# Two edits to a two-layer attention and expert network: expert inputs by a list of tokens per slot, and the turning of the near-bias table beside the first maxima

## The chip, the cores and the metric

The program runs on one core of a Trainium2 chip. Its time is the device time of one execution in microseconds (us); the time of the kernel before is 2062.14 us, the median of three runs (2062.14, 2062.99, 2052.34). The engines are TensorE (PE in the rows, PEld for its weight loads), VectorE (DVE), ScalarE (ACT), GpSimd (POOL) and SyncE (SP, which here issues DMAs); each runs its own stream of instructions in order, and they meet through semaphores.

## The reference

A network of two layers on x of shape (4, 1024, 128), 4096 tokens of 128 numbers. Layer 0 is a state-space scan and a dense mixture of 16 experts. Layer 1 is an attention with a relative-position bias and a second sublayer that holds a causal attention and a routed mixture of 16 experts. Cut to what the change touches:

```
# layer 1, attention: 16 heads of 8 numbers, bias by bucketed distance key - query
att = einsum('bhqd,bhkd->bhqk', q, k) / sqrt(8) + compute_bias(rel_emb, t, t)
o   = softmax(att) @ v;  out = o.reshape(b, t, 128) @ Wo.T

# layer 1, second sublayer, after its causal attention: T = 4096, E = 16, C = 2*ceil(T/E) = 512
hidden = resid + (ctx @ o_w + o_b)
xt     = layer_norm(hidden, ln2_w, ln2_b).reshape(T, 128)
logits = xt @ router_w;  probs = softmax(logits)
top1   = argmax(probs);  top2 = argmax(logits without top1)
loc1   = cumsum(m1) - 1; loc2 = cumsum(m2) - 1 + m1.sum()     # m1, m2: one-hot of top1, top2
m1, m2 = m1 * (loc1 < C), m2 * (loc2 < C)                     # over 512 a choice is dropped
xin    = einsum('tec,td->ecd', dispatch, xt)                  # (16, 512, 128): slots of the experts
h      = gelu(xin @ fc1_w + fc1_b)                            # 128 -> 512
eout   = (h @ fc2_w + fc2_b) * 0.8                            # 512 -> 128
moe    = einsum('tec,ecd->td', combine, eout)                 # g1*slot of top1 + g2*slot of top2
return hidden + moe                                           # then x + gate * this
```

## The kernel before

**The order of the program.** Modulate; scan; first mixture (from about 120 to 460 us); modulate; the biased attention, whose names begin with `ba_`; modulate; the causal attention, whose names begin with `ca_`; routing; the second mixture. Most stages are a Block: every engine has its own list in it, and the next Block begins for all of them together. `projection` has no Block of its own: it returns five functions (one per engine) that `attend` calls at the head of its own Block (`first.tensor(pe)` and so on).

**The biased attention.** `projection` runs over 8 chunks of 512 tokens. For each, TensorE computes q and k (L734) and v (L739) into PSUM, VectorE and ScalarE split q and k into three bfloat16 parts, and SyncE stores these in DRAM (`qk_parts`) and loads them back in another layout (`qop`, `kop`, loads at L833). The kernel applies the position bias as a factor on the exponentials: near the diagonal it comes from the table `rb_near` (128 rows by 16 heads by 384), and elsewhere it is constant. The table is built with its rows in reverse. `projection` turns it in 12 pieces of 512 columns: TensorE multiplies a piece by a flipped identity (L747) into PSUM bank 6 or 7, VectorE copies it back over itself (L810, semaphore `near_kept`), one or two pieces per chunk. At the end of the projection TensorE and GpSimd wait until all 12 are back.

`attend` first finds each row's maximum, then the scores. A "turn" of the maxima is one head group of one block of queries: two matmuls of 512 columns (L1149), a maximum by VectorE over both (L1234). 24 turns (`BEFORE_FIRST`) are put ahead of the first scores (L1175); after that a planner written in Python (`plan`) mixes the rest with the scores, the exponentials by ScalarE (L1267), GpSimd's product with `rb_near` (L1313) and the value matmuls (L1194). The maxima use banks 0 to 3, the scores 4 to 6, the values 7. The causal attention runs the same two functions, without table and turns.

**Routing (`route`, one Block).** VectorE makes layer-norm statistics; VectorE and ScalarE write the normalised rows `xt` (plain, without ln2's weight); TensorE turns them and multiplies by the router; VectorE finds the two choices, counts places with TensorE's help, and forms for each choice a row number `row` between 0 and 8191 (expert times 512 plus place), or a number above for a dropped one. The first choice's numbers are cast at L1705 into `cs_to` (semaphore `to_ready`), then the second's. ScalarE copies `xt` for the second choice (L1626); GpSimd writes a token's own result row into the 129th column of both copies (L1632). Then `send_copies` (L1725): GpSimd scatters 32 tiles of 128 rows for each choice, 64 indirect DMAs, into `expert_rows_in`, which has 129 columns and was zeroed in the first mixture. While it sends, VectorE makes the weights `g`, multiplies `hidden` by the gate and adds it to x (L1717, eight operations).

**Second mixture (`experts`, a Block of its own).** SyncE waits for all 64 sends and then loads the 512 rows of one expert after another, two in flight. TensorE turns the rows (L1830), multiplies up (L1839: 4 x (128x512)) and down (L1848: 16 pairs of 128x128); ScalarE applies gelu; VectorE takes the row numbers out of the 129th column and applies ln2 behind the turn, adds the second bias into `ex_eo` (L1918). In TensorE's order expert e+1's turn stands ahead of expert e's up, and expert e's down behind expert e+1's up. GpSimd gives each expert's 512 results back with four indirect scatters into `expert_rows_out` (L1769). Weights of an expert are 256 KB twice, loaded by SyncE two experts ahead. Behind the last give SyncE reads both results of each token back, ScalarE, VectorE and GpSimd weigh and add them, and SyncE stores the output.

Of the kernel before, what the change touches and what calls it, by code (L numbers as in the profile page):

```python
# [13 lines left out]
F32 = mybir.dt.float32  # L14
BF16 = mybir.dt.bfloat16
I32 = mybir.dt.int32
# [4 lines left out]
P = 128  # L21
# [20 lines left out]
CAP = 2 * (TOK // E)  # L42
KEEP = 1.0 - 0.2
# [339 lines left out]
def first_mixture(nc, k, m, by_distance):  # L383
# [8 lines left out]
    with ExitStack() as c:  # L392
# [39 lines left out]
        with nc.Block() as block:  # L432
            @block.sync
            def _(sp):
# [4 lines left out]
                sp.dma_start(k.rows_in[0:E * CAP, 0:D].rearrange("(p a) d -> p a d", p=P),  # L439
                             zero[:, 0:D].unsqueeze(1).broadcast_to([P, E * CAP // P, D])).then_inc(cleared, 16)  # L440
                sp.dma_start(k.rows_in[0:E * CAP, D:D + 1].bitcast(I32).rearrange("(p a) b -> p (a b)", p=P), m["unused_rows"],
                             allow_slow_non_contiguous=True).then_inc(cleared, 16)

# [7 lines left out]
                sp.wait_ge(cleared, (3 + 2) * 16)  # L451
# [224 lines left out]
def projection(nc, k, a):  # L676
# [10 lines left out]
    FLIPS = H * NEAR // CH  # L687
# [12 lines left out]
    def flips(i):  # L700

        return range(i * FLIPS // NCH, (i + 1) * FLIPS // NCH)

# [3 lines left out]
    if not a.causal:  # L707
        flipped, near_kept = nc.alloc_semaphore("rb_flipped"), nc.alloc_semaphore("rb_near_kept")
        near = a.near[:].rearrange("p h q -> p (h q)")

# [15 lines left out]
    def tensor(pe):  # L726
        pe.wait_ge(halved, 2)
        for i in range(NCH):
# [13 lines left out]
            if not a.causal:  # L742
# [10 lines left out]
        if not a.causal:  # L753
            pe.wait_ge(near_kept, FLIPS)

# [18 lines left out]
    def gpsimd(pool):  # L774
# [10 lines left out]
        if not a.causal:  # L785
            pool.wait_ge(near_kept, FLIPS)

    def vector(dve):
# [5 lines left out]
        for i in range(NCH):  # L794
# [12 lines left out]
            if not a.causal:  # L807
# [29 lines left out]
def attend(nc, k, a):  # L837
# [186 lines left out]
    with ExitStack() as c:  # L1024
# [25 lines left out]
        JOINS = 1 if causal else 2  # L1050

# [13 lines left out]
        with nc.Block() as block:  # L1065
# [58 lines left out]
            def _(pe):  # L1124
# [76 lines left out]

                for x in range(BEFORE_FIRST):
                    top_turn(x)

# [41 lines left out]
            def _(act):  # L1246
                first.scalar(act)

# [24 lines left out]
            def _(pool):  # L1273
# [44 lines left out]
                values(0)  # L1318
                for u in range(NU):
# [213 lines left out]
def route(nc, k, m, r):  # L1533
# [6 lines left out]
    with ExitStack() as c:  # L1540
        def sb(name, shape, dt=F32):
            return c.enter_context(nc.sbuf_tensor("ro_" + name, shape, dt))

        wr, trash, ids = r.wr, r.trash, r.ids
# [17 lines left out]
        ex_go, to_ready, ids_set, copied, gated_h = (  # L1562
            nc.alloc_semaphore("ro_" + n) for n in ("ex_go", "to_ready", "ids_set", "copied", "gated_h"))
# [9 lines left out]

        with nc.Block() as block:
            block.sync(r.loads)

            @block.tensor
            def _(pe):
                def turn(i):
# [3 lines left out]
                    for j in range(4):  # L1583
# [3 lines left out]
                        ins = nc.tensor.transpose(k.ps[:, i % 2, j * P:(j + 1) * P], r.xt[:, 0, t, 0:D], k.cst[:, C_ID:C_ID + P])  # L1587
# [11 lines left out]
                for i in range(2):  # L1599
# [4 lines left out]
                    ins.then_inc(counts, 1)  # L1604

            @block.scalar
            def _(act):
# [3 lines left out]
                for i in range(NCH + 1):  # L1611
                    if i < NCH:
                        for t in range(4 * i + 1, 4 * i + 4, 2):
                            nc.scalar.activation(r.xt[:, 0, t, 0:D], r.hidden[:, t, :], ACT.Identity, bias=col(shift, t),
# [7 lines left out]
                act.wait_ge(dve_plain, NT // 2)  # L1622
                act.wait_ge(act_plain, NT // 2)
                for b in range(B):
                    ts = slice(b * TB, (b + 1) * TB)
                    nc.scalar.copy(r.xt[:, 1, ts, 0:D], r.xt[:, 0, ts, 0:D]).then_inc(copied, 1)  # L1626

            @block.gpsimd
            def _(pool):
                pool.wait_ge(loaded, 48)  # L1630
                for i in range(2):
                    nc.gpsimd.tensor_copy(r.xt[:, i, :, D:D + 1].bitcast(I32), ids[:, i, :].unsqueeze(2)).then_inc(ids_set, 1)  # L1632
                pool.wait_ge(ids_set, 2)
                pool.wait_ge(to_ready, 1)
                pool.wait_ge(dve_plain, NT // 2)
                pool.wait_ge(act_plain, NT // 2)
                send_copies(nc, k, r, 0)
                pool.wait_ge(to_ready, 2)
                pool.wait_ge(copied, B)
                send_copies(nc, k, r, 1)  # L1640

            @block.vector
            def _(dve):
# [4 lines left out]
                for t in range(0, NT, 2):  # L1648
                    vec.tensor_scalar(r.xt[:, 0, t, 0:D], r.hidden[:, t, :], col(mean, t), col(rstd, t),
# [26 lines left out]
                for i in range(2):  # L1676
# [28 lines left out]
                    vec.tensor_copy(r.to[:, i, :], row[:, i, :]).then_inc(to_ready, 1)  # L1705
# [6 lines left out]
                vec.tensor_tensor(r.g[:], r.g[:], col2[:].unsqueeze(1).broadcast_to([P, 2, NT]), ALU.mult)  # L1712
                dve.wait_ge(act_plain, NT // 2)
                for b in range(B):
                    h = r.hidden[:, b * TB:(b + 1) * TB, :]
                    xs = k.x[:, b * TB:(b + 1) * TB, :]
# [440 lines left out]
```

## Time and profile before

| | |
|---|---|
| median of three runs | 2062.14 us |
| profiled execution | 2056.92 us, span 2055.2 us |
| busy: PE, DVE, ACT, POOL | 1669.1 (81%), 1533.7 (75%), 1170.0 (57%), 847.3 us (41%) |
| instructions | 42001 |
| projection, biased attention | 476.8 to 509.4 us |
| its 24 first maxima | 509.4 to 535.9 us |
| projection, causal attention | 1245.5 to 1272.0 us |
| join of the causal heads | 1736 to 1756 us |
| routing; sends in it | 1756 to 1883 us; 1798.5 to 1883 us |
| experts' matmuls | 1889 to 2011 us |
| last give, end | 2020.84 us; 2055.2 us |

The shares of busy time are means over stages with different limits; a stage is read by the wait that ends last in it. A duration comes from one profiled execution. The granted clock of TensorE (PEclk) is a share of 2.4 GHz.

### The profile page before, as it was taken

Reading aid. Unit: us, or ns where it says so; the run is one execution under the profiler, and the core shown is the slowest. Engines: PE = TensorE matmul, PEld = TensorE weight load, DVE = VectorE, ACT = ScalarE, POOL = GpSimd, SP = SyncE. Lnnn points to the kernel's source line nnn. Section 1 sums busy time; section 2 is a strip of 40 time slices with the busy share of each in tenths; the row PEclk is TensorE's granted clock in tenths of the full one; section 3 lists DMA queues with packets and bytes.
Section 4 is the critical chain, followed back from the end, with each engine's and each line's share of the span. In section 5 each row is a group of like instructions: output and inputs, shape, how many; then the busy total and the mean of one; then the engine's idle time right before and its main releaser. Section 6 shows DMA issues by size and latency. Waiting matters only on the chain. (4 is left out here: it accounts for less than half of the span.)

```text
span 2055.2 us, 42001 instructions
## 1 busy us (share of the span) xinstructions
PE 1669.1 (81%) x15556; PEld 804.9 (39%) x15556; DVE 1533.7 (75%) x2709; ACT 1170.0 (57%) x2150; POOL 847.3 (41%) x1066
## 2 busy tenths in 40 slices
PE   5799999997799999999999627799999995501992
PEld 2666666664133333333332224233333332400771
DVE  4767888877899999999999367788888883550124
ACT  3232222225499898898988614577777774300332
POOL 1100000005488878778788525122121122074454
PEclk8789999998699999999999857799999998555996
DMA  2186000004101011001110035111111114111444
GB/s 80 63 139 88 0 0 0 0 0 144 32 21 37 20 22 37 20 22 31 26 21 5 23 87 150 38 38 34 36 32 38 39 23 98 48 48 51 138 134 143
DMA packets 96025, 103.06 MB, mean 50 GB/s; under 512 B 28288, under 2 KB 62800, under 8 KB 95344
## 3 DMA queue, kind: packets, MB, share of 16 engines
q1 hardware_dynamic: 91760, 92.33, 19.2%
q0 software_dynamic: 4096, 8.43, 1.2%
q8 instruction: 112, 1.84, 0.4%
q14 instruction: 57, 0.47, 0.1%
HBM read 63.65 MB, written 36.80 MB: 49 GB/s over the span
## 5 line engine op out<-in xcount | busy, mean ns | idle before, releaser
L1234 DVE TENSOR_REDUCE ba_at_top<-ps 128x2 f32<-128x1024 f32 x512 | 588.4, 1217 | 18.0 <-PE ps L1149 16.2
L1267 ACT ACTIVATE ba_at_ring<-ps 128x512 f32<-128x512 f32 x1024 | 556.9, 597 | 64.8 <-PE ps L1175 51.4
L1313 POOL TENSOR_TENSOR ba_at_ring<-ba_at_ring,rb_near 128x256 f32<-128x256 f32 (+2 forms) x640 | 483.2, 783 | 148.2 <-ACT ba_at_ring L1267 142.3
L1234 DVE TENSOR_REDUCE ca_at_top<-ps 128x2 f32<-128x1024 f32 (+3 forms) x384 | 348.6, 954 | 68.6 <-PE ps L1149 33.0
L1267 ACT ACTIVATE ca_at_ring<-ps 128x512 f32<-128x512 f32 (+1 forms) x640 | 318.7, 553 | 98.7 <-PE ps L1175 96.6
L1175 PE MATMUL ps<-qop,kop 49*128 49x512 bf16 (+3 forms) x1792 | 321.6, 367 | 35.2 <-DMA qop<-ca_at_negm 7.2
L1149 PE MATMUL ps<-kop,qop 48*128 48x512 bf16 (+3 forms) x1792 | 316.7, 368 | 32.2 <-DVE ba_at_top L1234 12.4
L1194 PE MATMUL ps<-ba_at_ring,ba_at_low 128*32 128x256 f32 (+1 forms) x4864 | 329.6, 358 | 12.7 <-ACT ba_at_osb L1254 9.8
L1303 POOL TENSOR_SCALAR_AFFINE_SELECT ca_at_ring<-ca_at_ring 128x512 f32<-128x512 f32 x128 | 80.0, 637 | 359.3 <-ACT ca_at_ring L1267 359.2
L520 ACT ACTIVATE gm_sg<-ps,gm_bias 128x512 f32<-128x512 f32 x128 | 88.1, 688 | 235.0 <-PE ps L460 235.0
L1175 PEld LDWEIGHTS ps<-qop,kop 49*128 49x128 bf16 x1792 | 81.5, 93 | 351.2 <-ACT ba_at_ring L1267 189.0
L1194 PE MATMUL ps<-ca_at_ring,ca_at_low 128*32 128x256 f32 (+1 forms) x2816 | 192.1, 354 | 13.5 <-issue 8.5
L1194 PEld LDWEIGHTS ps<-ba_at_ring,ba_at_low 128*32 128x32 f32 x4864 | 103.8, 108 | 170.4 <-issue 106.0
L604 DVE SCALAR_TENSOR_TENSOR gm_y<-ps,gm_w,gm_y 128x128 f32 (+1 forms) x512 | 144.0, 344 | 31.0 <-DVE gm_bef L377 16.9
L466 PEld LDWEIGHTS ps<-gm_w,gm_hc 128*128 128x128 f32 x1024 | 134.5, 192 | 62.6 <-issue 47.7
L652 POOL TENSOR_TENSOR gm_gated<-gm_y,row 128x512 f32 x8 | 10.1, 1266 | 350.2 <-DVE gm_y L604 350.2
L1149 PEld LDWEIGHTS ps<-kop,qop 48*128 48x128 bf16 x1792 | 95.6, 94 | 130.3 <-issue 42.2
L466 PE MATMUL ps<-gm_w,gm_hc 128*128 128x128 f32 x1024 | 135.4, 275 | 0.7 <-DVE gm_hc L592 0.7
L459 PE MATMUL ps<-hT,gm_w 128*128 (+1 forms) x256 | 133.5, 604 | 0.0
L460 PE MATMUL ps<-hT,gm_w 128*128 (+1 forms) x256 | 132.5, 599 | 0.0
L592 DVE SCALAR_TENSOR_TENSOR gm_hc<-ps,gm_bias,gm_sg 128x512 f32<-128x512 f32 x128 | 95.6, 747 | 43.6 <-ACT gm_sg L520 43.0
L1769 POOL DMA_INDIRECT expert_rows_out<-ex_eo,ex_to x64 | 61.4, 960 | 77.3 <-DVE ex_eo L1918 62.4
(316 smaller groups left out, 1728.6 us busy)
## 6 DMA issues: line engine op xcount, KB each, us to landing
cs_fc<-in_fc_w SPq DMA_DIRECT2D x32, 256.0 KB, 2.7
qk_parts<-ba_at_ring SPq DMA_DIRECT2D x24, 256.0 KB, 3.7
qop<-qk_parts SPq DMA_DIRECT2D x64, 96.0 KB
kop<-qk_parts SPq DMA_DIRECT2D x64, 96.0 KB
qk_parts<-ca_at_ring SPq DMA_DIRECT2D x24, 256.0 KB, 3.6
ex_xi<-expert_rows_in SPq DMA_DIRECT2D x16, 258.0 KB, 3.1
expert_rows_in<-gm_zero SPq DMA_DIRECT2D x1, 4096.0 KB
expert_rows_out<-gm_zero SPq DMA_DIRECT2D x1, 4096.0 KB
```

The lines of the kernel that those rows point to most:

```text
L459: nc.tensor.matmul(k.ps[:, A + e % 2, :], w1[:, e, :], k.hT[:, tok], start=True, stop=True)
L460: nc.tensor.matmul(k.ps[:, C + e % 2, :], w3[:, e, :], k.hT[:, tok], start=True, stop=True).then_inc(up, 1)
L466: ins = nc.tensor.matmul(k.ps[:, O + e % 2, j * P:(j + 1) * P], hc[:, e % 2, j * P:(j + 1) * P], w2[:, e, :], start=True, stop=True)
L520: nc.scalar.activation(sg[:, e % 2, :], k.ps[:, A + e % 2, :], ACT.Silu, bias=bias[:, 0, e:e + 1]).then_inc(silu, 1)
L592: nc.vector.scalar_tensor_tensor(hc[:, e % 2, :], k.ps[:, C + e % 2, :], bias[:, 1, e:e + 1], sg[:, e % 2, :], ALU.add, ALU.mult).then_inc ...
L604: ins = nc.vector.scalar_tensor_tensor(yt, k.ps[:, O + e % 2, j * P:(j + 1) * P], w[:, t, e], yt, ALU.mult, ALU.add)
L1149: ins = nc.tensor.matmul(k.ps[:, slot + s, 0:k1 - k0], qop[rows, g, pair, i * P:(i + 1) * P], kop[rows, g, pair, k0:k1], start=True, stop= ...
L1175: ins = nc.tensor.matmul(k.ps[:, B_BANK + bank_of(u, t + s), at:at + q1 - q0], kop[rows, g, pair, i * P:(i + 1) * P], qop[rows, g, pair, q ...
L1194: ins = nc.tensor.matmul(k.ps[32 * j:32 * j + 32, O_BANK, s0 - half * CH:s1 - half * CH], vs[:, u % 2, var, i, j, :], ring[:, ring_of(u, n ...
L1234: nc.vector.tensor_reduce(top[:, k0 // CH, half, :, pair, i % HB], k.ps[:, slot:slot + 2, 0:k1 - k0], AX.X, ALU.max).then_inc(a_read, 1)
L1267: nc.scalar.activation(ring[:, ring_of(u, n) * HG + t % HG, 0:width(n)], k.ps[:, B_BANK + bank_of(u, t), 0:width(n)], ACT.Exp).then_inc(ex ...
L1313: ins = nc.gpsimd.tensor_tensor(w, w, a.near[:, u % NG * HG + j, lo - (i - 1) * P:hi - (i - 1) * P], ALU.mult)
```

## The change

**The table.** The 12 turns leave `projection`. In `attend` TensorE issues one turn behind every second of the 24 first maxima, into the score banks 4 to 6 in rotation, and ScalarE copies the piece back, behind its part of the projection. TensorE waits for all 12 behind the 24th maximum; GpSimd waits behind its first value tiles.

**The expert inputs.** Nothing is sent. SyncE stores the plain rows `xt` once into `expert_rows_in` (now 4096 rows of 128), four DMAs. For each choice VectorE splits the row number into slot tile (number >> 7; there are 64 tiles) and place in the tile (number & 127) and compares both with a running index: `ids` (128 x 32 x 64, bfloat16) and `same` (128 x 32 x 128, bfloat16). ScalarE writes `ids` times (partition + 1), GpSimd multiplies `ids` by the token tile's number, and TensorE sums over all tokens, 64 matmuls of 128x128 into bank 7: for each slot the tile and partition of its token. Seven small operations of VectorE make two lists of it, `rows[:, 1]` (the token to fetch) and `rows[:, 0]` (the result row to write). GpSimd fetches an expert's rows with four indirect gathers into one of four buffers, and gives with four scatters. Fetches run three experts ahead of gives.

**Beside these.** Experts join routing's Block. Their loops are written out instead of looped by register. The gate times `hidden`, added to x, moves from routing's VectorE list into the expert loop (behind experts 3, 6, 9 and 12). The zero store of `expert_rows_in` in the first mixture and the 129th column are gone.

```diff
 projection
-            if not a.causal:
-                for f in flips(i):
-                    if f >= 2:
-                        pe.wait_ge(near_kept, f - 1)
-                    nc.tensor.matmul(k.ps[:, 6 + f % 2, :], k.cst[:, C_FLIP:C_FLIP + P], near[:, f * CH:(f + 1) * CH],
-                                     start=True, stop=True).then_inc(flipped, 1)
...
-                for f in flips(i):
-                    dve.wait_ge(flipped, f + 1)
-                    nc.vector.tensor_copy(near[:, f * CH:(f + 1) * CH], k.ps[:, 6 + f % 2, :]).then_inc(near_kept, 1)
 attend
+                def flip(f):
+                    if f >= NBANK:
+                        pe.wait_ge(near_kept, f - NBANK + 1)
+                    nc.tensor.matmul(k.ps[:, B_BANK + f % NBANK, :], k.cst[:, C_FLIP:C_FLIP + P],
+                                     near_flat[:, f * CH:(f + 1) * CH], start=True, stop=True).then_inc(flipped, 1)
                 for x in range(BEFORE_FIRST):
                     top_turn(x)
+                    if x % 2 and x // 2 < FLIPS:
+                        flip(x // 2)
+                if FLIPS:
+                    pe.wait_ge(near_kept, FLIPS)
...
                 first.scalar(act)
+                for f in range(FLIPS):
+                    act.wait_ge(flipped, f + 1)
+                    nc.scalar.copy(near_flat[:, f * CH:(f + 1) * CH], k.ps[:, B_BANK + f % NBANK, :]).then_inc(near_kept, 1)
 route
+                for b in range(B):                                                     # SyncE
+                    sp.wait_ge(dve_plain, (b + 1) * TB // 2)
+                    sp.wait_ge(act_plain, (b + 1) * TB // 2)
+                    sp.dma_start(k.rows_in[b * L:(b + 1) * L, :].rearrange("(t p) d -> p t d", p=P),
+                                 r.xt[:, b * TB:(b + 1) * TB, :]).then_inc(r.sent, 16)
...
+                for i in range(2):                                                     # TensorE
+                    pe.wait_ge(weighed, i + 1)
+                    pe.wait_ge(by_tile, i + 1)
+                    for t in range(NT):
+                        ins = nc.tensor.matmul(k.ps[:, 7, 0:2 * NSLOT], same[:, i, t, :],
+                                               ids[:, i, t, :, :].rearrange("p o c -> p (o c)"),
+                                               start=i == 0 and t == 0, stop=i == 1 and t == NT - 1)
...
+                    nc.scalar.activation(ids[:, i, :, 1, :], ids[:, i, :, 0, :], ACT.Copy,
+                                         scale=rc[:, T_PART:T_PART + 1]).then_inc(weighed, 1)
...
-                send_copies(nc, k, r, 0)
-                pool.wait_ge(to_ready, 2)
-                pool.wait_ge(copied, B)
-                send_copies(nc, k, r, 1)
+                    nc.gpsimd.tensor_tensor(ids[:, i, :, 0, :], ids[:, i, :, 0, :], tile, ALU.mult).then_inc(by_tile, 1)
...
-                    vec.tensor_copy(r.to[:, i, :], row[:, i, :]).then_inc(to_ready, 1)
+                    L_(vec.tensor_copy(numi[:, 0, :], row[:, i, :]))
+                    L_(vec.tensor_scalar(numi[:, 1, :], numi[:, 0, :], 7, None, ALU.logical_shift_right))
+                    L_(vec.tensor_scalar(numi[:, 2, :], numi[:, 0, :], P - 1, None, ALU.bitwise_and))
+                    L_(vec.tensor_copy(numf[:], numi[:, 1:3, :]))
+                    vec.tensor_tensor(ids[:, i, :, 0, :], rc[:, T_IOTA:T_IOTA + NSLOT].unsqueeze(1).broadcast_to([P, NT, NSLOT]),
+                                      numf[:, 0, :].unsqueeze(2).broadcast_to([P, NT, NSLOT]), ALU.is_equal)
+                    vec.tensor_tensor(same[:, i, :, :], rc[:, T_IOTA:T_IOTA + P].unsqueeze(1).broadcast_to([P, NT, P]),
+                                      numf[:, 1, :].unsqueeze(2).broadcast_to([P, NT, P]), ALU.is_equal).then_inc(alike, 1)
 experts
+        def fetch(e):
+            if e >= XB:                                                                # XB = OB = 4
+                pool.wait_ge(turned, e - XB + 1)
+            for q in range(QT):
+                at = e * QT + q
+                nc.gpsimd.indirect_dma_start(xi[:, e % XB, q, :], None, k.rows_in,
+                                             bass.IndirectOffsetOnAxis(ap=r.rows[:, 1, at:at + 1], axis=0)).then_inc(x_in[e % XB], 16)
+        def give(e):
+            pool.wait_ge(eo_ready, e + 1)
+            for q in range(QT):
+                at = e * QT + q
+                nc.gpsimd.indirect_dma_start(k.rows_out, bass.IndirectOffsetOnAxis(ap=r.rows[:, 0, at:at + 1], axis=0),
+                                             eo[:, e % OB, q, :], None).then_inc(eo_out[e % OB], 16)
+        pool.wait_ge(r.table_ready, 1)
+        pool.wait_ge(r.sent, B * 16)
+        for e in range(XB - 1):
+            fetch(e)
+        for e in range(E):
+            if e + XB - 1 < E:
+                fetch(e + XB - 1)
+            give(e)
```

On TensorE, from the last chunks of the biased projection to the first scores, before (`rb_near,cst` is a turn, `kop,qop` the maxima, `qop,kop` the scores):

```order
L734 MATMUL ps<-hT,ba_w 128x512 x2
L739 MATMUL ps<-ba_w,hT 128x128 x4
L747 MATMUL ps<-rb_near,cst 128x512 x2
L1149 MATMUL ps<-kop,qop 128x512 x36
L1137 MATMUL ps<-cst,ba_at_top 16x128
L1149 MATMUL ps<-kop,qop 128x512 x12
L1175 MATMUL ps<-qop,kop 128x512 x6
```

The same place after:

```order
L721 MATMUL ps<-hT,ba_w 128x512 x2
L726 MATMUL ps<-ba_w,hT 128x128 x4
L1125 MATMUL ps<-kop,qop 128x512 x4
L1182 MATMUL ps<-rb_near,cst 128x512
L1125 MATMUL ps<-kop,qop 128x512 x4
L1182 MATMUL ps<-rb_near,cst 128x512
...
L1125 MATMUL ps<-kop,qop 128x512 x4
L1182 MATMUL ps<-rb_near,cst 128x512
L1125 MATMUL ps<-kop,qop 128x512 x2
L1151 MATMUL ps<-qop,kop 128x512 x6
```

The turns moved from the ends of the chunks to behind every fourth matmul of the maxima, and the last stands two matmuls ahead of the scores.

On GpSimd, from routing to the sum, before (`cs_to` and `ex_to` are row numbers):

```order
L1632 COPY cs_xt<-cs_ids 128x32 x2
L1725 DMA expert_rows_in<-cs_xt,cs_to 16384x129 x64
L1574 UNCONDITIONAL_BRANCH
L1764 UNCONDITIONAL_BRANCH
L1769 DMA expert_rows_out<-ex_eo,ex_to 16384x128 x64
L1776 TENSOR_TENSOR qop<-qop,row 128x512 x8
```

The same place after (`cs_rows` holds both lists):

```order
L1653 TENSOR_TENSOR qop<-qop,cs_route_consts 128x32x64 x2
L1788 DMA ex_xi<-expert_rows_in,cs_rows 128x128 x16
L1795 DMA expert_rows_out<-ex_eo,cs_rows 16384x128 x4
L1788 DMA ex_xi<-expert_rows_in,cs_rows 128x128 x4
L1795 DMA expert_rows_out<-ex_eo,cs_rows 16384x128 x4
...
L1788 DMA ex_xi<-expert_rows_in,cs_rows 128x128 x4
L1795 DMA expert_rows_out<-ex_eo,cs_rows 16384x128 x16
L1811 TENSOR_TENSOR qop<-qop,row 128x512 x8
```

The 64 scatters ahead of the experts are gone; 64 gathers stand among the 64 gives in one queue, four experts' worth ahead of the first give, and four experts' gives are left behind the last gather.

## Rows read from the trace of the kernel before

**Rows 1.** Chain of waits, experts and last give (start us, us, what).
```profile
1891.59 1.13 PE ps L1830 x4
...
1893.97 5.80 PE ps L1839 x8
1899.77 0.44 PE ps L1830 x4
1900.20 3.44 PE ps L1839 x8
1903.64 3.57 PE ps L1848 x32
...
2011.02 0.70 DVE ex_eo L1918
2011.72 0.27 issue
...
2020.84 2.25 DMA expert_rows_out<-ex_eo,ex_to
```
**Rows 2.** The sends, L1725 (ns min/median/max, starts; idle us, times).
```profile
L1725 POOL DMA_INDIRECT expert_rows_in<-cs_xt,cs_to x64: 957/962/1962, 1798.5 to 1882.1; - x64
  issue: 19.2, 63
```
**Rows 3.** Timeline, both projections (start us, us, operation, idle before and its releaser).
```profile
476.78 1.99 PE L734 MATMUL ps<-hT,ba_w 128*128 128x512 f32 x4 [1.47 <-DVE ba_bias L791]
...
509.41 0.61 PE L1149 MATMUL ps<-kop,qop 48*128 48x512 bf16 x4 [1.19 <-DVE rb_near L810]
...
1245.53 1.98 PE L734 MATMUL ps<-hT,ca_w 128*128 128x512 f32 x4 [1.47 <-DVE ca_bias L791]
...
1271.99 0.29 PE L1149 MATMUL ps<-kop,qop 48*128 48x128 bf16 x2 [4.11 <-DMA kop<-qk_parts]
...
1280.06 1.05 SPq L833 DMA_DIRECT2D qop<-qk_parts  x3
```
**Rows 4.** Timeline, a turn of the table and the first maxima.
```profile
479.49 1.02 PE L747 MATMUL ps<-rb_near,cst 128*128 128x512 f32 x2
...
518.90 9.13 DVE L1234 TENSOR_REDUCE ba_at_top<-ps 128x2 f32<-128x1024 f32 x8
...
535.90 0.61 PE L1149 MATMUL ps<-kop,qop 48*128 48x512 bf16 x2 [0.52 <-DVE ba_at_top L1234]
536.30 0.64 PE L1175 MATMUL ps<-qop,kop 49*128 49x512 bf16 x2
```
**Rows 5.** Timeline, operations like the new ones.
```profile
1272.05 0.44 PE L1159 MATMUL ps<-half 64*128 64x128 bf16 x4
...
1731.35 4.43 DVE L1986 TENSOR_TENSOR cs_h<-cs_h,cs_ob 128x4096 f32<-128x4096 f32 x1 [0.81 <-DMA ca_jo_wo<-in_ca_wo]
...
1740.94 2.35 POOL L1392 TENSOR_TENSOR ca_jo_num<-ca_jo_num,ca_jo_den 128x1024 f32<-128x1024 f32 x1 [18.78 <-DMA ca_jo_num<-head_sums]
...
1759.30 0.52 POOL L1632 COPY cs_xt<-cs_ids 128x32 int32<-128x32 int32 x2 [7.64 <-DMA cs_ids<-in_result_rows]
...
1782.05 3.87 ACT L1626 COPY cs_xt<-cs_xt 128x1024 f32<-128x1024 f32 x4
...
1814.01 0.18 DVE L1705 CAST cs_to<-ro_row 128x32 int32<-128x32 f32 x1
...
1821.53 1.21 DVE L1717 TENSOR_TENSOR cs_h<-cs_h,row 128x1024 f32<-128x1024 f32 x1
```
**Rows 6.** Busy time by stretch, causal join (us, busy (x) per engine, PEclk, DMA share, GB/s).
```profile
1741.00:1744.00 3.00, 1.16 (x8) 0.97 (x8) 2.24 (x9) 0.00 (x0) 2.29 (x1) 0.96 1.05 244
1744.00:1747.00 3.00, 1.95 (x13) 1.65 (x11) 1.70 (x5) 0.00 (x0) 1.79 (x1) 0.61 1.04 250
1747.00:1750.00 3.00, 2.38 (x11) 2.38 (x12) 1.50 (x8) 0.00 (x0) 1.26 (x2) 0.50 0.28 71
1750.00:1753.00 3.00, 2.69 (x18) 2.39 (x18) 1.98 (x7) 0.00 (x0) 1.66 (x1) 0.75 0.00 0
```

More of the change, by code:

```diff
@@ L42 @@
 CAP = 2 * (TOK // E)
+NSLOT = E * CAP // P
 KEEP = 1.0 - 0.2
@@ new lines, in experts, with gpsimd @@
+    x_in = [nc.alloc_semaphore(f"ex_x_in{s}") for s in range(XB)]
+    eo_out = [nc.alloc_semaphore(f"ex_eo_out{s}") for s in range(OB)]
+    got = [nc.alloc_semaphore(f"ex_got{s}") for s in range(4)]
+    first, both, gated, summed, x_stored, gated_h, x_plain = (
+        nc.alloc_semaphore("ex_" + n) for n in ("first", "both", "gated", "summed", "x_stored", "gated_h", "x_plain"))
+    def gpsimd(pool):
+        def fetch(e):
[19 more added lines that the diff above has]
+            give(e)
+        for n in range(NCH):
+            pool.wait_ge(both, 4 * (n + 1))
+            y = back[:, 1, n % 4, :, :]
+            b = n * CH // L
+            nc.gpsimd.tensor_tensor(y, y, k.row[:, 2, b:b + 1, :].broadcast_to([P, 4, D]), ALU.mult).then_inc(gated, 1)
@@ new lines, in sync @@
+    def sync(sp):
+        for e in range(E - 2):
+            sp.wait_ge(up, (e + 1) * FB)
+            load_first(sp, m, r, e + 2, e % 2)
+            sp.wait_ge(down, e + 1)
+            load_second(sp, m, r, e + 2, e % 2)
+        for s in range(OB):
+            sp.wait_ge(eo_out[s], E // OB * QT * 16)
+        for n in range(NCH):
+            if n >= 4:
+                sp.wait_ge(summed, n - 3)
+            for i in range(2):
+                sp.dma_start(back[:, i, n % 4, :, :], k.rows_out[i * TOK + n * CH:i * TOK + (n + 1) * CH, :]
+                             .rearrange("(j p) d -> p j d", p=P)).then_inc(got[n % 4], 16)
+        x_out = m["out"].rearrange("b (t p) d -> p (b t) d", p=P)
+        for n in range(NCH):
+            sp.wait_ge(summed, n + 1)
+            sp.dma_start(x_out[:, 4 * n:4 * n + 4, :], k.x[:, 4 * n:4 * n + 4, :]).then_inc(x_stored, 16)
+        sp.wait_ge(x_stored, NCH * 16)
@@ new lines, in tensor, with turn, upper, lower @@
+    def tensor(pe):
+        def turn(e):
+            pe.wait_ge(x_in[e % XB], QT * 16 * (e // XB + 1))
+            if e >= 2:
+                pe.wait_ge(xT_ready, e - 1)
+            for q in range(QT):
+                ins = nc.tensor.transpose(k.ps[:, e % 2, q * P:(q + 1) * P], xi[:, e % XB, q, :], k.cst[:, C_ID:C_ID + P])
+            ins.then_inc(turned, 1)
+        def upper(e):
+            pe.wait_ge(r.first_in[e % 2], 16 * (e // 2 + 1))
+            pe.wait_ge(xT_ready, e + 1)
+            for f in range(FB):
+                if e:
+                    pe.wait_ge(act_done, e * FB + f - (FB - 1))
+                nc.tensor.matmul(k.ps[:, 2 + f, :], fc1[:, e % 2, f * P:(f + 1) * P], xT[:, e % 2, :], start=True, stop=True).then_inc(up, 1)
+        def lower(e):
+            pe.wait_ge(r.second_in[e % 2], 16 * (e // 2 + 1))
+            pe.wait_ge(act_done, (e + 1) * FB)
+            if e >= 2:
+                pe.wait_ge(eo_ready, e - 1)
+            for q in range(QT):
+                for f in range(FB):
+                    ins = nc.tensor.matmul(k.ps[:, 6 + e % 2, q * P:(q + 1) * P], hh[:, e % 2, f, q * P:(q + 1) * P], fc2[:, e % 2, f, :],
+                                           start=(f == 0), stop=(f == FB - 1))
+            ins.then_inc(down, 1)
+        turn(0)
+        for e in range(E):
+            if e + 1 < E:
+                turn(e + 1)
+            upper(e)
+            if e:
+                lower(e - 1)
+        lower(E - 1)
@@ new lines, in scalar @@
+    def scalar(act):
+        act.wait_ge(consts_in, 32)
+        for e in range(E):
+            for f in range(FB):
+                act.wait_ge(up, e * FB + f + 1)
+                if f == 0 and e >= 2:
+                    act.wait_ge(down, e - 1)
+                nc.scalar.activation(hh[:, e % 2, f, :], k.ps[:, 2 + f, :], ACT.Gelu, bias=b1[:, e, f:f + 1]).then_inc(act_done, 1)
+        act.wait_ge(r.g_ready, 1)
+        for t in range(NT):
+            n = t // 4
+            if t % 4 == 0:
+                act.wait_ge(got[n % 4], (n // 4 + 1) * 2 * 16)
+            y1 = back[:, 0, n % 4, t % 4, :]
+            nc.scalar.activation(y1, y1, ACT.Copy, scale=r.g[:, 0, t:t + 1]).then_inc(first, 1)
@@ L2010, in causal_sublayer @@
         route(nc, k, m, r)
-        experts(nc, k, m, r)
 def program(nc, m):
```

350 lines of the change are left out of this document (114 added, 236 removed).

## The prediction

> **What bounds the kernel now.** I read the times by stage, then the chain of waits, then the timeline around the places that the diff touches. The chain ends in the experts: every expert is turned (0.44 us), multiplied up (3.44) and down (3.57) with no idle time between, 7.45 us of TensorE for each of 16 experts, and behind the last one come eight indirect DMAs of GpSimd, the last of which starts at 2020.84 [rows 1]. Ahead of the experts TensorE stands still: GpSimd issues 64 scattered copies, the first at 1798.5, the last at 1882.1, one every 0.96 + 19.2/63 = 1.265 us [rows 2], and the first expert begins only at 1891.59. So the last sublayer is GpSimd's descriptor writing first and TensorE's matmuls second, one after the other. The other place of the diff is the projection of the biased attention. It has a twin in this program, the causal attention's, which runs the same code without the bias table; so what the table costs there can be read by comparing the two [rows 3].
>
> **The bias table.** The biased projection takes 509.41 − 476.78 = 32.63 us from its first matmul to the first maximum, its twin 1271.99 − 1245.53 = 26.46 [rows 3]. The 12 turns with their VectorE copies thus cost 6.2 us, and that goes.
> What comes instead lies beside the first 24 maxima. These are paced by VectorE, 9.13/8 = 1.14 us each [rows 4]. One turn is a pair of matmuls, 1.02 us with its pipeline end [rows 4], 0.86 in a stream at full clock and 1.7 at half. TensorE spends 0.61 on a maximum at half clock [rows 4], so two maxima leave it 2.28 − 1.22 = 1.06: enough at full clock, 0.65 too little at half clock, and the twin starts its maxima at half clock after a pause. With the turns in it TensorE has no pause left, so I let the clock rise after two such pairs: 1.3 us. ScalarE can copy only after it has seen the projection's stores land, in the twin 8.07 us after the first maximum, when the next load goes out [rows 3]; the fourth turn, behind the eighth maximum, wants the first copy at 7 × 1.14 = 8.0. That is 0.2 us at most, together 1.5. Behind the last maximum stand one turn (0.86), one copy by ScalarE (0.97 at 1024 elements by 3.87/4 [rows 5], so 0.6 to 0.7 at 512) and a wait of 0.2, where now the scores start 0.40 us after it (535.90 to 536.30 [rows 4]): 1.4. Sum −6.2 + 1.5 + 1.4 = −3.3 us. All of it, −6.2, is one bound; the other is 0, if the clock stays low through all twelve turns.
>
> **Until the first fetch.** VectorE now makes, for each of the two choices, the two halves of a token's row number (four small operations like the cast that they replace, 0.18 [rows 5], with their waits 0.8 us more than now) and two comparisons, 128x2048 and 128x4096. Elementwise rows of two inputs: 1.21 us at 1024 elements, 4.43 at 4096 [rows 5], so 1.05 ns an element, 2.28 at 2048. That is 0.8 + 2.3 + 4.4 = 7.5 us a choice; the first choice delays the second. The second choice's row numbers come at 1814.0 [rows 5], hence the comparisons end at 1814.0 + 7.5 + 7.6 = 1829.1. Then in series, each on one engine with nobody to hide it: ScalarE's copy of 2048 elements, twice a 1024 copy of 3.87/4 (1.9, with the wait 2.0) [rows 5]; GpSimd's product, twice 2.35 (4.7) [rows 5]; 32 small matmuls at 0.44/4 (3.5, with the wait 3.7) [rows 5]; VectorE's seven small operations on the table (0.18 each and upwards, with waits 1.8) and GpSimd's wake-up (0.3). First fetch at 1842. Bounds 1838 and 1850: the products may overlap a little, or the broadcast operands may run slower than the rows. The four plain stores of the token rows are long landed by then.
>
> **The fetches and gives.** GpSimd now issues 64 gathers and 64 scatters in one queue: three experts fetched, then one fetch and one give in turn. No gather is in the trace. The nearest row is the scatter, 0.957 at least and 1.962 at most [rows 2]; a small copy of the same engine, 0.26, is the lower end [rows 5]. I take the scatter's 1.265 with its gap, since the number of rows per DMA is the same. Then 128 DMAs, the last starting 127 × 1.265 = 160.7 us after the first: 2002.7, if GpSimd never waits. Now it is 2020.84: 18 us less. But it waits.
> At the start: the first expert's matmuls stand behind the turn of the second, whose fourth gather starts at 1842 + 7 × 1.265 = 1850.9 and lands 2.25 later (as the last scatter [rows 1]). Turn 0.5, up 5.80 as the first one now at half clock, turn 0.44, up 3.44, down 3.57, VectorE 0.70, wake-up 0.27 [rows 1]: 1867.9. GpSimd is free at 1842 + 16 × 1.265 = 1862.2: 5.7 us.
> In the loop: the give of expert e needs the turn of expert e + 2. From the end of that fetch: landing 1.0, turn, up, down, VectorE, wake-up (0.44 + 3.44 + 3.57 + 0.70 + 0.27), 9.4 us. GpSimd has 8 × 1.265 = 10.1 of its own to do in that time, so nothing is late at full clock, and TensorE idles 10.1 − 7.45 = 2.7 us per expert. That idling decides. In the join of the heads TensorE works in bursts with pauses of under 2 us, and the granted clock (1.00 is 2.4 GHz, 0.50 is 1.2) goes 0.96, 0.61, 0.50 over three stretches in which it is busy 1.16, 1.95 and 2.38 of 3 us [rows 6]. So I expect each pause to drop the clock from 2.4 to 1.2 GHz, and a matmul stretch to lose what the first one loses now, 5.80 − 3.44 = 2.4. Path 11.8, with 0.3 for a gather that contends with the weights 12.1: 2.0 late. The fetch two experts on moves with it, the neighbour then has slack, so every second expert pays: six of the twelve that still have a fetch behind them, 12 us.
> At the end only gives are left, 5.06 an expert against TensorE's 7.45: two experts 2.4 late, 5 us.
> Together 5.7 + 12 + 5 = 22.7, last give at 2025.4, 4.6 us later than now. What follows it (the reading back and the sum) is the same code.
> The residual's eight VectorE operations move from beside the sends to beside the fetches. Such a meeting costs GpSimd at most 1.0 us (a send of 1.962 against the median of 0.962 [rows 2]), and the median says that few sends met one: I take 1.5 us, for sends then and for fetches now, so no change. The Trainium skill has a stronger rule (SBUF — State Buffer, Who interferes with whom): a VectorE operation with two SBUF inputs and a GpSimd operation that reads SBUF shut each other out for the whole instruction. By it eight operations of 1.21 us [rows 5] would cost up to 9.7 in the loop, by the rows 1.5; the trace bears out that the two meet, not that each meets for its whole length.
> The dropped zero stores and the unrolled expert loops lie beside TensorE's work in the first mixture and behind prefetch; I cost them at nothing, a microsecond if I am wrong.
>
> **Sum.** −3.3 + 4.6 = +1.3 us on the profiled execution's 2056.92: 2058. The median of the runs shown is 5 us above that execution, its runs 2052 to 2063, so 2058 stands for both within their scatter.
>
> **Rivals.**
> Clock holds (28%). The pauses are 2.7 of 10.1 us, and the bursts are longer than in the join; for it speaks that a stretch that is busy 2.69 of 3 us already brings the clock back to 0.75 [rows 6]. Then the 12 us are gone, the end costs 6: last give at 2014.4, −6.4, with the table −9.7: 2047.
> [...]
> The gather is dearer (17%), the slower side. It sits on GpSimd's queue, 64 times, and GpSimd is the bound. At 0.35 us more (1.31, as the sends beside VectorE) the gathers add 22 us; some 9 go into waits that exist anyway. Last give 2038, 2070 in all. It decides from about 0.22 us. Against it: the same number of descriptors.
> The turns gain nothing (5%): the stores hold the maxima back as long as the table did. 2061.
>
> **How the numbers follow.** Forecast 50%, own range 2049 to 2068 (bounds of the first fetch −4 and +8, table −6.2 to 0). A measurement here tells 0.5%, 10 us, from no change. Faster: half of the first rival's, a cheaper gather and the forecast's lower edge, 0.28; slower: the gather's 17% and the upper edge, 0.21; the same 0.51. Range 2040 (clock holds and table in full, cheaper gather) to 2075.
>
> **What would show it.** The first maximum 6 us earlier; the first gather at 1836 (1842 less the gain); gathers of 0.96; granted clock falling in the expert loop and up-stretches of 5 us among those of 3.44; last give within 5 us of now. Wrong if the expert loop runs at 1.00 throughout, or if a gather takes over 1.2 us.

## Result: the change loses 0.1 to 0.3 per cent, and the profile after

The changed kernel took 2062.34 us (median of 12 runs), the kernel before 2058.93 (12 runs): ratio 1.0027, 95% interval 1.0014 to 1.0040, so 3 to 8 us slower. Its profiled execution took 2061.27 us (span 2059.6), against 2056.92 (2055.2). A second measurement (below) gave 1.0013, 1.0004 to 1.0022. Both intervals lie above 1, so the loss is small and clear of the noise.

I cut both spans at five places and put beside them the lists alone and the second measurement, both described below:

| us, from the profiles | before | after | after again | lists alone | forecast |
|---|---|---|---|---|---|
| start to first projection matmul | 476.8 | 477.9 | 476.3 | 476.1 | 476.8 |
| to the first score | 59.5 | 55.6 | 55.3 | 59.5 | 56.2 |
| to the start of routing | 1220.4 | 1220.9 | 1220.0 | 1219.9 | 1220.4 |
| start of routing to first fetch | | 86.2 | 86.5 | 86.4 | 85.3 |
| first fetch to last give | | 186.6 | 188.4 | 187.3 | 183.4 |
| start of routing to last give | 264.2 | 272.8 | 274.8 | 273.7 | 268.7 |
| last give to the end | 34.4 | 32.6 | 32.4 | 32.4 | 34.4 |

Two of these stretches carry the change: the table wins 4 us, the lists lose 9 to 11. Some 2 us come back behind the last give.

**The table.** The timeline of the changed kernel, from the projection to the first score (start us, us, operation, idle before it):

```profile
477.86 1.98 PE L721 MATMUL ps<-hT,ba_w 128*128 128x512 f32 x4 [1.47 <-DVE ba_bias L767]
...
504.71 1.04 PE L1125 MATMUL ps<-kop,qop 48*128 48x512 bf16 x4 [4.63 <-DVE ba_v L782]
...
505.68 2.08 PE L1182 MATMUL ps<-rb_near,cst 128*128 128x512 f32 x2
...
508.33 2.36 DVE L1221 TENSOR_REDUCE ba_at_top<-ps 128x2 f32<-128x1024 f32 x2 [0.62 <-PE ps L1125]
...
512.16 1.56 ACT L1237 COPY rb_near<-ps 128x512 f32<-128x512 f32 x3 [7.55 <-DMA qk_parts<-ba_at_ring]
...
531.61 1.12 PE L1182 MATMUL ps<-rb_near,cst 128*128 128x512 f32 x2
...
532.67 0.39 PE L1125 MATMUL ps<-kop,qop 48*128 48x512 bf16 x2
...
532.77 0.59 ACT L1237 COPY rb_near<-ps 128x512 f32<-128x512 f32 x1 [1.92 <-PE ps L1182]
533.41 0.39 PE L1151 MATMUL ps<-qop,kop 49*128 49x512 bf16 x2 [0.36 <-ACT rb_near L1237]
```

The projection has become 26.85 us long, as its causal twin, where it was 32.63 [rows 3]; from there to the first score it is 28.70, where it was 26.89. Of the 5.8 us 1.8 go back. The first two turns run near half clock (2.08 and 1.84 us, granted clock 0.50 and 0.64) and hold up VectorE's maxima by 0.62 and 0.17; from the first maximum to the last it takes 1.5 us more than before. The last turn (531.61) stands ahead of the 24th maximum (532.67), not behind it, and only the wait for its copy, 0.34 us more than before, lies between that maximum and the first score.

**Routing.** Its start in both kernels is ScalarE's table load, and the two products of GpSimd with what VectorE did beside them (timeline; before first, then after):

```profile
1756.68 1.28 ACT L1609 ACT_TABLE_LOAD   x1 [32.92 <-PEq L1348]
```

```profile
1754.27 1.28 ACT L1629 ACT_TABLE_LOAD   x1 [32.99 <-PEq L1340]
...
1804.54 3.63 POOL L1653 TENSOR_TENSOR qop<-qop,cs_route_consts 128x2048 bf16<-128x2048 bf16 x1 [56.65 <-ACT qop L1644]
1805.23 3.48 DVE L1683 TENSOR_TENSOR ro_c<-ro_l,ro_col 128x512 f32<-128x512 f32 x1
...
1821.70 0.18 DVE L1719 CAST ro_numi<-ro_row 128x32 int32<-128x32 f32 x1
...
1831.32 3.62 POOL L1653 TENSOR_TENSOR qop<-qop,cs_route_consts 128x2048 bf16<-128x2048 bf16 x1 [23.15 <-ACT qop L1644]
1831.39 3.58 DVE L1732 TENSOR_SCALAR ro_col<-ro_col 128x32 f32<-128x32 f32 x1
1835.08 3.28 PE L1620 MATMUL ps<-qop,kop 128*128 128x128 bf16 x32 [19.23 <-POOL qop L1653]
...
1840.45 1.19 POOL L1788 DMA_INDIRECT ex_xi<-expert_rows_in,cs_rows  x1 [5.52 <-DVE cs_rows L1743]
```

The second choice's row numbers come 67.4 us after the start of routing, 57.3 in the kernel before (1814.01 [rows 5]). A comparison of 512 elements that takes 0.69 elsewhere in this chain took 3.48, and it ended half a microsecond behind GpSimd's product.

**The experts.** What the gives waited for, from their line (ns min/median/max, starts; idle us, times), and the chain of waits over two experts (start us, us, what):

```profile
L1795 POOL DMA_INDIRECT expert_rows_out<-ex_eo,cs_rows x64: 963/970/1725, 1866.0 to 2027.0; - x64
  DVE ex_eo L1903: 25.2, 9
```

```profile
1956.50 1.73 POOL expert_rows_out L1795
...
1964.93 0.94 POOL ex_xi L1788
1966.17 2.52 DMA ex_xi<-expert_rows_in,cs_rows
1968.74 1.11 PE ps L1840 x4
1969.86 5.78 PE ps L1849 x8
1975.64 3.59 PE ps L1858 x32
1979.25 0.70 DVE ex_eo L1903
1980.22 0.99 POOL expert_rows_out L1795
```

Before, the chain ran through TensorE expert by expert with 7.45 us each [rows 1]. Now it goes round: gather, landing, turn, up mostly at half clock (5.78 for 3.44), down, VectorE, give. The granted clock in that up and in the down behind it (busy (x) of PE, PEld, DVE, ACT, POOL; PEclk; DMA share; GB/s):

```profile
1970.00:1972.00 2.00, 2.00 (x3) 0.67 (x2) 0.70 (x1) 0.40 (x1) 1.68 (x2) 0.50 0.19 66
1975.60:1979.00 3.40, 3.40 (x33) 3.40 (x31) 0.00 (x0) 0.69 (x1) 1.40 (x2) 1.00 0.19 52
```

GpSimd is idle for 25.2 us in nine places: 5.6 ahead of the first give, 13.2 in six waits in the loop, 6.3 in two at the end. Each of the nine contains the 0.30 us that stands between any two of its DMAs, so the waiting proper is 22.5 us. Without it the queue takes 164.1 us. One of its DMAs beside one of the residual's VectorE operations (timeline):

```profile
1956.14 1.22 DVE L1908 TENSOR_TENSOR cs_h<-cs_h,row 128x1024 f32<-128x1024 f32 x1
1956.50 1.73 POOL L1795 DMA_INDIRECT expert_rows_out<-ex_eo,cs_rows  x1 [2.50 <-DVE ex_eo L1903]
```

### The profile page after: what moved, and what is told of

Read it like the earlier page. It is cut to its first block and busy times, and to the rows that moved or that the text cites. A ratio compares the mean times of both kernels' runs of the same rounds, so it can differ in the third digit from the quotient of the medians.

```text
span 2059.6 us, 41745 instructions
## 1 busy us (share of the span) xinstructions
PE 1693.5 (82%) x15620; PEld 815.4 (40%) x15620; DVE 1546.1 (75%) x2698; ACT 1175.8 (57%) x2160; POOL 852.1 (41%) x1066
## 3 DMA queue, kind: packets, MB, share of 16 engines
q0 software_dynamic: 4096, 8.40, 1.3%
## 5 line engine op out<-in xcount | busy, mean ns | idle before, releaser
L1151 PE MATMUL ps<-qop,kop 49*128 49x512 bf16 (+3 forms) x1792 | 322.6, 368 | 34.4 <-DMA qop<-ca_at_negm 7.1
L648 POOL TENSOR_TENSOR gm_gated<-gm_y,row 128x512 f32 x8 | 10.1, 1266 | 350.9 <-DVE gm_y L600 350.9
L1878 ACT ACTIVATE hT<-ps,cs_b 128x512 f32<-128x512 f32 x64 | 43.6, 687 | 114.5 <-PE ps L1849 114.5
```

Of the source, the lines that this page charges most:

```text
L1151: ins = nc.tensor.matmul(k.ps[:, B_BANK + bank_of(u, t + s), at:at + q1 - q0], kop[rows, g, pair, i * P:(i + 1) * P], qop[rows, g, pair, q ...
```

## Experiments

My theory of the loss: the lists lose what the table wins, because the 64 gathers and 64 gives of one queue start late and wait 25 us. Each ratio is against the kernel before, timed beside the experiment.

**The table alone.** The kernel before with only the projection's and `attend`'s lines of the change.

```diff
-                    nc.tensor.matmul(k.ps[:, 6 + f % 2, :], k.cst[:, C_FLIP:C_FLIP + P], near[:, f * CH:(f + 1) * CH],
...
+                    if x % 2 and x // 2 < FLIPS:
+                        flip(x // 2)
```

> The kernel before with the table's turns moved beside the first maxima, and nothing else of the change. Theory: the gain of the projection is kept, first score 3 to 4 us earlier, the whole 3 to 6 us shorter than before (ratio 0.997 to 0.9985). Rival: the attention takes it back, since VectorE's maxima pace it; ratio 1.000.

2054.78 us against 2057.38: ratio 0.9988 (0.9979 to 0.9996), a little less gain than expected. In the profile 55.4 us from the first projection matmul (477.79) to the first score (533.23), 4.1 less than before. The table's gain is kept, 1 to 4 us of it in the runs.

**The lists alone.** The changed kernel with the turns back in the projection.

```diff
-                    if x % 2 and x // 2 < FLIPS:
-                        flip(x // 2)
+            if not a.causal:                       # projection, as before
+                for f in flips(i): ...
```

> The changed kernel with the turns back in the projection: the lists alone. Theory: the lists are what costs. Routing runs 10 us longer up to the second choice's row numbers and the last give starts 8 to 10 us later than before; ratio 1.003 to 1.005. Rival: the lists cost nothing and the slower time is scatter of the attention stages; ratio 1.000 and a last give within 2 us of before, counted from the start of routing.

2067.7 us: ratio 1.0056 (1.0043 to 1.0069), somewhat above what I had expected. From the start of routing (1755.55) to the last give (2029.23) 273.7 us, 9.5 more than before. The lists are what costs. Table and lists measured apart add up to 1.0044 with an uncertainty of some 0.0015; the two measurements of the whole, 1.0027 and 1.0013, lie below that, and whether the parts help each other stays open.

**Six buffers.** Four fetch buffers mean that GpSimd stands three experts ahead of its gives.

```diff
-    XB, OB = 4, 4
+    XB, OB = 6, 4
```

> The changed kernel with six fetch buffers instead of four: GpSimd fetches five experts ahead of the give, nothing else. Theory: GpSimd's queue of 128 descriptor writings is the bound and its 25 us of waits come from gives that stand too close behind a fetch. With two more fetches between them the waits go: last give starts 127 x 1.265 = 161 us after the first fetch instead of 186.6, the whole 20 to 25 us shorter than the changed kernel (2037 to 2042). Rival: TensorE with its half-clock stretches is the bound and the waits only show its pace; then the last give moves by the 6 us at the end at most (2056 or more).

2039.15 us: ratio 0.9909 (0.9895 to 0.9924), 0.9% faster than before with everything else of the change as it is. GpSimd's first gather, the only give that VectorE releases, and its last give (timeline):

```profile
1840.19 1.19 POOL L1788 DMA_INDIRECT ex_xi<-expert_rows_in,cs_rows  x1 [5.81 <-DVE cs_rows L1743]
...
1932.91 1.63 POOL L1795 DMA_INDIRECT expert_rows_out<-ex_eo,cs_rows  x1 [0.30 <-DVE ex_eo L1903]
...
2004.30 0.97 POOL L1795 DMA_INDIRECT expert_rows_out<-ex_eo,cs_rows  x1 [0.30 <-issue]
```

The one idle time put down to VectorE is the ordinary 0.30, so no wait is left. From first fetch to last give it takes 164.1 us, where 161 were computed: four DMAs beside the residual took 1.63 to 1.70 us, and the first one 1.19. TensorE still falls to half clock behind its pauses here (ups of 4.7 to 6.0 us in five experts); it no longer matters, since GpSimd does not wait for it. The rival, TensorE as the bound, falls.

**Five buffers**, and the changed kernel once more:

```diff
-    XB, OB = 4, 4
+    XB, OB = 5, 4
```

> The changed kernel with five fetch buffers instead of four (six gave 20 us). Theory of the queue: between the last gather of an expert and the give that needs it stand 9 DMAs with four buffers (9 x 1.27 = 11.4 us, against a path of 11.2 us at full clock and 13.6 to 14.1 behind a pause) and 17 with five (21.6 us). So one more buffer already takes all waits in the loop, and most of the first and of the last ones: last give 161 to 165 us after the first fetch, the whole as with six buffers, ratio 0.990 to 0.993. Rival: each further buffer takes a part of the waits; then five lie halfway between four and six, last give some 175 us after the first fetch, ratio 0.996 or above.

2044.06 us: ratio 0.993 (0.9916 to 0.9943). All waits of GpSimd for a result:

```profile
1872.06 1.00 POOL L1795 DMA_INDIRECT expert_rows_out<-ex_eo,cs_rows  x1 [1.39 <-DVE ex_eo L1903]
...
1998.42 0.97 POOL L1795 DMA_INDIRECT expert_rows_out<-ex_eo,cs_rows  x1 [2.43 <-DVE ex_eo L1903]
...
2005.43 0.96 POOL L1795 DMA_INDIRECT expert_rows_out<-ex_eo,cs_rows  x1 [2.22 <-DVE ex_eo L1903]
```

The loop's six waits are gone with one buffer more, as the count of DMAs between an expert's last gather and the give that needs it says. The first wait (1.4) and the end (4.7) remain in part; last give 168.6 us after the first fetch, 3.6 more than I had expected at most.

> The changed kernel itself, once more beside the kernel before, for the size of its loss and for a second profile. If the loss is the steps seen so far (about 4 us won by the table, 8 to 9 lost from the start of routing to the last give, 1 to 2 won behind it): ratio 1.001 to 1.003 and 270 to 275 us from the start of routing to the last give, where before has 264. If the first measurement was scatter: 1.000 or less, or another length of that stretch.

2060.13 us: ratio 1.0013 (1.0004 to 1.0022); 274.8 us from the start of routing to the last give. As the steps say, and no scatter.

**TensorE kept busy.** Filler matmuls while TensorE waits for a gather.

```diff
+            for _ in range((5, 3)[e] if e < 2 else 2):
+                nc.tensor.matmul(k.ps[:, e % 2, :], k.cst[:, C_ID:C_ID + P], k.cst[:, 0:CH], start=True, stop=True)
             pe.wait_ge(x_in[e % XB], QT * 16 * (e // XB + 1))
```

> The changed kernel with filler matmuls on TensorE (two of 512 columns, 0.86 us each at full clock) ahead of each expert's turn, five and three ahead of the first two; their results are overwritten. Theory of the clock: the loop's waits (2.4, 2.8, 1.3, 2.5, 2.9, 1.3 us) come from the up-stretch at half clock behind TensorE's pause; with the pause partly filled they go or halve, last give 7 to 12 us earlier than in the changed kernel (2050 to 2055). Rival: the gathers' landing of 2.5 us makes them; the waits stay above 12 us in sum, 2062 or more.

2061.39 us: ratio 1.0009 (0.9995 to 1.0022), not to be told from the changed kernel without fillers. The granted clock rose, as the stretches of 40 us show (busy (x) of PE, PEld, DVE, ACT, POOL; PEclk; DMA share; GB/s). After:

```profile
1881.00:1921.00 40.00, 31.92 (x170) 22.54 (x168) 9.13 (x11) 10.30 (x15) 27.20 (x28) 0.90 0.29 93
1921.00:1961.00 40.00, 31.47 (x158) 21.59 (x159) 8.18 (x10) 10.99 (x16) 28.06 (x29) 0.91 0.28 91
```

With fillers, then that kernel's long ups and GpSimd's waits in the loop:

```profile
1889.00:1929.00 40.00, 35.86 (x190) 24.16 (x189) 9.11 (x11) 10.38 (x16) 29.74 (x30) 1.00 0.30 96
1929.00:1969.00 40.00, 35.05 (x174) 22.88 (x173) 8.30 (x10) 11.00 (x16) 29.45 (x30) 0.96 0.28 91
```

```profile
1895.50 1.72 POOL L1795 DMA_INDIRECT expert_rows_out<-ex_eo,cs_rows  x1 [0.97 <-DVE ex_eo L1905]
1927.61 1.72 POOL L1795 DMA_INDIRECT expert_rows_out<-ex_eo,cs_rows  x1 [1.06 <-DVE ex_eo L1905]
1940.29 5.29 PE L1851 MATMUL ps<-ex_xT,cs_fc 128*128 128x512 f32 x8
1950.16 1.00 POOL L1795 DMA_INDIRECT expert_rows_out<-ex_eo,cs_rows  x1 [1.72 <-DVE ex_eo L1905]
1974.55 5.29 PE L1851 MATMUL ps<-ex_xT,cs_fc 128*128 128x512 f32 x8
1984.42 1.00 POOL L1795 DMA_INDIRECT expert_rows_out<-ex_eo,cs_rows  x1 [2.98 <-DVE ex_eo L1905]
```

The loop's waits fall from 13.2 to 6.7 us, and the two longest are those behind the two ups that still ran half at 1.2 GHz; so the clock makes about half of the loop's waits, and the rival, the landing alone, falls too. But my figure of 7 to 12 us was missed: from first fetch to last give 184.0 us, only 2.6 less than after. The first wait stayed at 5.9, and the two at the end grew from 6.3 to 8.2. I put that down to the fillers' own time on TensorE, which no run separates.

**One product less on GpSimd.** The first choice's product in 32 small operations of ScalarE, the second's as it was.

```diff
+                        for t in range(NT):
+                            ins = nc.scalar.activation(ids[:, 0, t, 0, :], ids[:, 0, t, 0, :], ACT.Copy, scale=float(t))
-                for i in range(2):                 # GpSimd's products
+                for i in range(1, 2):
```

> The changed kernel with the first choice's product (ids times token tile) made by ScalarE in 32 small operations instead of GpSimd's one; the second choice's stays on GpSimd. Theory: GpSimd's product shuts VectorE's two-input operation L1683 out for its whole length (3.48 us instead of 0.69). Then that comparison takes 0.69 again, the second choice's row numbers come 64.6 us after the start of routing instead of 67.4, and VectorE's small operation beside the second product stays long (3.6 us). Rival: VectorE is slow there for another reason (ScalarE's copy of 2048 elements, or the operation's own operands); it stays at 3.5 us.

One run, 2057.29 us; its profile tells:

```profile
1750.85 1.28 ACT L1630 ACT_TABLE_LOAD   x1 [34.42 <-PEq L1340]
...
1801.78 0.69 DVE L1689 TENSOR_TENSOR ro_c<-ro_l,ro_col 128x512 f32<-128x512 f32 x1
...
1815.45 0.18 DVE L1725 CAST ro_numi<-ro_row 128x32 int32<-128x32 f32 x1
...
1825.06 3.62 POOL L1659 TENSOR_TENSOR qop<-qop,cs_route_consts 128x2048 bf16<-128x2048 bf16 x1 [80.39 <-ACT qop L1645]
1825.14 3.59 DVE L1738 TENSOR_SCALAR ro_col<-ro_col 128x32 f32<-128x32 f32 x1
```

The comparison takes 0.69 again, the second row numbers come 64.6 us after the start of routing, 2.8 earlier, and VectorE's small operation beside the product that stayed takes 3.59. GpSimd's product shuts VectorE out: shown. ScalarE was at work beside the comparison here too, so the rival, ScalarE's copy, falls.

**All together.** Six buffers, both products on VectorE, the residual in VectorE's idle time ahead of the logits (operands shortened).

```diff
+                    vec.tensor_tensor(hot[:], iota, tile_number, ALU.is_equal).then_inc(alike, 1)
+                    vec.tensor_tensor(same[:, i, :, :], iota, place, ALU.is_equal)
+                    vec.tensor_tensor(ids[:, i, :, 0, :], hot[:], token_tile, ALU.mult).then_inc(by_tile, 1)
-                    nc.gpsimd.tensor_tensor(ids[:, i, :, 0, :], ids[:, i, :, 0, :], tile, ALU.mult).then_inc(by_tile, 1)
-                if e % 3 == 0 and e // 3 <= B:
-                    residual(e // 3 - 1)           # now ahead of the router's logits
```

> The changed kernel with six fetch buffers, both products on VectorE (reading a one-hot that is kept apart, so that ScalarE's weighing runs beside the second comparison), and gate times hidden added to x in VectorE's idle time ahead of the router's logits instead of in the expert loop. Theory: beside the 20 to 25 us of the six buffers, first fetch 3 to 4 us earlier (two us of ScalarE and 3.6 of GpSimd leave the path, 2.3 of VectorE come in; the first choice's product costs VectorE 2.3 where it was shut out for 2.8), and the fetches lose no 2.6 us to VectorE any more: 2030 to 2036, ratio 0.986 to 0.990. Rival: TensorE's pace takes over behind a faster queue; then no more than the six buffers alone gave, ratio 0.991.

2035.76 us: ratio 0.9894 (0.9872 to 0.9917), 1.1% faster than the kernel before. The runs alone do not tell it from the six buffers (0.9895 to 0.9924); the profile does.

```profile
1752.07 1.28 ACT L1632 ACT_TABLE_LOAD   x1 [33.53 <-PEq L1340]
...
1834.17 1.19 POOL L1800 DMA_INDIRECT ex_xi<-expert_rows_in,cs_rows  x1 [87.40 <-DVE cs_rows L1755]
...
1995.66 0.97 POOL L1807 DMA_INDIRECT expert_rows_out<-ex_eo,cs_rows  x1 [0.30 <-issue]
```

First fetch 82.1 us after the start of routing (86.2 after), and 161.5 from there to the last give (164.1 with six buffers alone): 127 x 1.27, GpSimd's DMAs one behind the other with 0.30 us between them, none but the first longer than 1.00. At that price of a DMA it is the bound of this way of doing it.

## Why the prediction was right or wrong

**The table: right, with one place misread.** −4.0 us measured, −3.3 forecast. The gain is as computed (5.8 against 6.2), and the maxima are held up by 1.5 us as forecast. Behind the last maximum I had put a turn and its copy, 1.4 us; the last turn stands ahead of that maximum, and 0.34 came in. So 1.8 us went back instead of 2.9.

**First fetch: right within a microsecond by luck, from two errors that cancel.** 85.3 forecast, 86.2 measured. I expected VectorE's work to run beside GpSimd's product undisturbed and the product to take 4.7 us. It took 3.62, but the first one cost VectorE 2.8. The Trainium skill (SBUF — State Buffer, Who interferes with whom) says that VectorE with two SBUF inputs and a GpSimd operation that reads SBUF shut each other out, and that `tensor_scalar` can take the shared ports too; the 3.48 and 3.58 us above agree. I had weighed that rule for the residual only, and made 9.7 us of it. The same section infers that `tensor_tensor` does not stall GpSimd's descriptor generation, which would make nothing of it. The measurement lies between: of 128 indirect DMAs four in the loop took 1.43 to 1.73 us, 2.6 us together above the others; with the residual moved away none did.

**Fetches and gives: the mechanism right, one term too small. This is the step that failed.** Forecast 183.4 us from first fetch to last give, measured 186.6, 188.4 and 187.3 (after, after again, lists alone). The term is GpSimd's own time for its 128 DMAs: 160.7 forecast, 164.1, 164.6 and 164.3 measured, and 164.1 with six buffers, where nothing waits. The waits were forecast at 22.7 and measured, without the ordinary 0.30 in each, at 22.5, 23.7 and 23.0. The price of 1.265 us a DMA was the median send with its gap. The starts in [rows 2] give more, 83.6/63 = 1.327, for the first send and seven others took 1.14 to 1.96 us. I set the meetings with the residual at 1.5 us for sends and fetches alike, "so no change"; that holds for a difference from the kernel before, but the sum was built up from 1842, and there they were put at nothing. They cost 2.6 to 3.0 us, and the first gather another 0.2. With the residual moved away the queue took 161.5. This split is an account of the trace: a DMA that is lengthened inside the loop can shorten the wait behind it.

That the waits came out in sum is partly luck. The first was 5.3 to 5.7 us against 5.7, the six of the loop 11.4, 13.5 and 13.3 against 12, the end 5.7, 4.5 and 4.2 against 5. Every second expert pays, as forecast, but between 1.0 and 2.9 us each instead of 2.0. I had a gather land 1.0 us behind its writing; it lands 2.5 us behind its start, hence 1.25. And TensorE does not pause 2.7 us in each expert: in the first profile its long pauses in the loop stand in every second expert, 4.3 to 5.5 us, with the clock down to 0.50 behind the one shown and the ups behind them at 4.5 to 6.0 us.

**The number that the sum was let stand for: the second step that failed.** The terms added up to slower by 1.3, yet I let 2058 stand for the median of three runs as well, 2062.14; read against that it said faster, and the change is slower. Twelve runs of before have their median at 2058.93, 3.2 us below that of the three shown. A sum of terms belongs on top of the median that it is compared with: 2060.2 here, against 2062.34 measured.

**The rivals.** Clock holds: no, and the fillers show what it would have been worth, half of the loop's waits; with the fillers' own time in the path 2.6 us of it were left. A dearer gather: no, 0.947 us against the scatter's 0.970. The turns gain nothing: no. What none of them held: how far the waits hang on one number of the source. I worked out that 10.1 us of queue stand against a path of 11.8, and did not ask how many DMAs a buffer more would put between; eight are worth 10 us of queue and end the waits.

Behind the last give the changed kernel is 1.8 to 2.0 us shorter. The last sum comes 27.9 us behind that give in both. The difference is GpSimd's DRAIN instruction at the end of its last Block, behind which the program ends: 6.99 us before (L1763), 5.04 after (L1577). It took 5.04 in the lists alone too, 6.02 with five buffers and 7.00 with six, so the kernels that wait less lose up to 2 us of their gain again there; what sets its length stays open. Open, too, is why the stretch between first score and routing, in which no line was changed, varies by 3 us among eight of the profiles and was 3 and 7 us longer than the longest of these with five buffers and with fillers.

## What to carry to other kernels

When work moves into a queue that another engine feeds and drains, count the entries between the one that starts a piece and the one that waits for it, and compare their time with the path of the piece at its slowest: here 9 x 1.27 us against 11.2 to 14, and one buffer more was worth more than the whole change. Price such a queue by its whole length over its entries too, since the median entry leaves out the long ones. The change exchanged 64 sends for 64 gathers and won their overlap with TensorE; it gave that back by starting the queue 86 us into routing instead of 42. And where GpSimd gets an elementwise product beside VectorE's serial chain, price it on VectorE first.

## What the runs showed that I had not expected

A VectorE operation of 32 columns (L1732; the same operation takes 0.18 us in the last kernel, which has no product on GpSimd) took 3.58 us beside GpSimd's product of 2048, ending with it; a reduction of 512 elements that began with the first product took its usual 0.69. And the half-clock stretches that lengthen the path go on in the kernels with five and six buffers; eight indirect DMAs more between a gather and its give are enough to hide them in the loop.
